# Attention logits of a graph kernel drawn for seven steps at once

## The reference, cut to what matters

```
a = h[src] @ Ws.T + h[dst] @ Wd.T + emb_rel[etype] @ Wr.T
e = leaky_relu((a @ attn_fc2_w.T)[:, 0], 0.01)
m = segment_max(e, dst)
w = exp(e - m[dst])
alpha = w / segment_sum(w, dst)[dst]
agg = segment_sum(alpha[:, None] * h[src], dst)
```

## Time and profile before

| | us |
|---|---|
| median of 3 runs | 11182.82 (11172.02 to 11192.22) |
| the profiled execution | 11168.36 |
| its span, first to last instruction | 11166.6 |
| attention, from its first one-hot to its last addition's start | 7414.1 to 9960.2 |
| attention, steady part | 2527.3 |
| busy in the steady part: TensorE, VectorE, ScalarE, GpSimd | 2308, 2230, 1950, 1547 |

### The profile page before, as it was taken

How to read it: one execution, slowest core, us unless ns; L and a number is a source line. 1 busy time by engine, 2 the same in 40 slices (tenths; PEclk the granted TensorE clock), 3 DMA queues, 4 the chain that set the end, 5 groups by cost and what they waited for, 6 DMA issues and landing times.

```text
span 11166.6 us, 189255 instructions
## 1 busy us (share of the span) xinstructions
PE 8637.6 (77%) x45271; PEld 6646.5 (60%) x45271; DVE 7796.6 (70%) x26977; ACT 6047.5 (54%) x18738; POOL 7800.5 (70%) x7060
## 2 busy tenths in 40 slices
PE   3344555555578899988898999989999999967888
PEld 2233333333346677677777778767777777745665
DVE  5677454455486677755664444778888888889999
ACT  6854555555585666611110000767777777766665
POOL 0088887778718888888865888846666666649995
PEclk6555555555589999999999999975555555557776
DMA  2111111111167888899996777321111111110000
GB/s 47 20 49 41 43 43 44 45 44 43 45 204 196 204 218 218 210 276 246 244 257 223 227 232 223 48 57 46 46 46 46 46 46 46 46 46 6 1 1 24
DMA packets 656014, 1170.95 MB, mean 105 GB/s; under 512 B 140942, under 2 KB 565074, under 8 KB 632158
## 3 DMA queue, kind: packets, MB, share of 16 engines
q0 software_dynamic: 363536, 437.35, 20.4%
q10 hardware_dynamic: 25344, 574.83, 13.4%
q1 hardware_dynamic: 266062, 146.67, 5.2%
HBM read 885.82 MB, written 278.99 MB: 104 GB/s over the span
## 4 chain that ended last, share of the span: by engine, by line
POOL 31%; PE 23%; ACT 15%; issue 14%; DVE 12%; DMA 2%; DVEq 2%; SPq 1%; ACTq 0%; POOLq 0%
POOL step_data L1388 12%; POOL onehot L2075 9%; PE bank L987 8%; PE bank L1349 7%; POOL step_data L1660 6%; ACT onehot L974 5%; POOL gather_ring L1388 4%; ACT onehot L976 3%; DVE step_small L1895 2%; ACT keys L580 2%; PE bank L1935 2%; PE bank L1943 1%; ACT step_small L1972 1%; DVE arena L1883 1%; DVE keys L1908 1%
## 5 line engine op out<-in xcount | busy, mean ns | idle before, releaser
L962 POOL DMA_INDIRECT gather_ring<-mean_rows,step_data x1660 | 2045.0, 1232 | 902.4 <-DVE arena L759 396.9
L987 PE MATMUL bank<-gather_ring,onehot 128*128 128x130 f32 x3320 | 1252.5, 484 | 1244.5 <-ACT onehot L976 490.9
L1349 PE MATMUL bank<-arena 128*128 128x384 bf16 x9506 | 1797.7, 329 | 25.4 <-DMA arena<-split_out 24.2
L987 PEld LDWEIGHTS bank<-gather_ring,onehot 128*128 128x128 f32 x3320 | 833.8, 313 | 1650.5 <-ACT onehot L976 655.5
L1349 PE MATMUL bank<-arena,keys 128*128 128x384 bf16 x9408 | 1791.8, 330 | 9.5 <-DMA arena<-split_im 9.5
L1388 POOL DMA_INDIRECT step_data<-hidden,window_idx x960 | 1553.1, 1618 | 316.6 <-issue 291.5
L1349 PEld LDWEIGHTS bank<-arena 128*128 128x128 bf16 x9506 | 1307.3, 138 | 328.3 <-issue 41.3
L1349 PEld LDWEIGHTS bank<-arena,keys 128*128 128x128 bf16 x9408 | 1294.5, 138 | 318.1 <-issue 34.9
L1660 POOL DMA_INDIRECT step_data<-next_rows,window_idx x672 | 1117.4, 1663 | 344.8 <-issue 313.1
L1020 DVE TENSOR_TENSOR arena<-arena,bank 128x130 f32 x1660 | 480.8, 290 | 1125.8 <-PE bank L987 1027.5
L1866 POOL DMA_INDIRECT gather_ring<-attention_rows,step_data x834 | 786.3, 943 | 605.9 <-DVE step_small L1919 460.7
(11 more groups left out here) (310 smaller groups left out, 20200.2 us busy)
## 6 DMA issues: line engine op xcount, KB each, us to landing
keys<-count_rows ACTq DMA_DIRECT2D x56, 3136.0 KB
arena<-count_rows ACTq DMA_DIRECT2D x56, 3136.0 KB
count_rows<-arena ACTq DMA_DIRECT2D x29, 3136.0 KB
count_rows<-keys ACTq DMA_DIRECT2D x29, 3136.0 KB
gather_ring<-mean_rows,step_data POOLq DMA_INDIRECT x1660, 2.5
step_data<-hidden,window_idx POOLq DMA_INDIRECT x960
gather_ring<-attention_rows,step_data POOLq DMA_INDIRECT x834, 2.5
keys<-attention_rows,step_data POOLq DMA_INDIRECT x826, 2.5
```

The lines of the kernel that those rows point to most:

```text
L962: e.indirect_dma_start(ring_at(rings.slot(name, i), SUM_COLS, SUMS - 1), None, rows, bass.IndirectOffsetOnAxis(src_idx[:, i:i + 1], 0), bo ...
L987: e.matmul(pass_bank[i % N_SUM_BANKS][:, 0:SUMS], onehot[:, i % STEP_SLOTS, :], ring_at(rings.slot(name, i), SUM_COLS, SUMS), start=True, ...
L1349: m = e.matmul(pass_bank[n % 2][:, 0:SPLIT_COLS], counts[t % 2][:, :, h], split[:, h, :], start=(h == 0), stop=(h == NODE_TILES - 1))
```

## The change

Seven steps share one draw of logits. The product of `nodes_hot` (hop 3) has three columns a step, one for each bf16 piece, and goes to the step's own three columns of one PSUM bank that holds the scores of seven steps. After the seventh step's product, `draw_vector` (hop 4, every seventh step) adds the three pieces with one reduction over 128x7x3, adds the relation scores and the source scores of seven steps, and takes the leaky ReLU; the two copies of coefficients stand in it as well. The later stages move back by twelve half-steps (the mask from hop 5 to 17, the addition from 15 to 27), since the first of seven steps now waits for the last. `edges_hot` gets 16 slots. PSUM is divided: the transposes of hop 1 alternate between two banks, the seven steps' scores have one, and the later half of the pipeline (transposes and sums) goes round five; TensorE waits for the copy of two steps back and the addition of five steps back. Gathers signal by groups of seven, and GpSimd waits for the sum of 28 steps back and the coefficients' copies alone. The diff, cut to its core:

```diff
-                             ("attention", GATHER_SLOTS, [1] * STEPS)))
+                             ("attention", ATTENTION_SLOTS // DRAWN,
+                              [min(DRAWN, STEPS - g * DRAWN) for g in range(DRAWS)])))
...
-    HOPS = 16
+    HOPS = 28
+    DRAW_STEPS = 4
+    drawn = small[:, 0:4, 0:DRAWN]
...
+    HALF_BANKS, LATE_BANKS = 2, 5
...
+    def dst_scores(n):
+        return bank_all[HALF_BANKS][:, 0:PIECES * n].rearrange("p (s k) -> p s k", k=PIECES)
...
     def attention_gpsimd(e):
...
-            if j >= GATHER_SLOTS:
-                e.wait_ge(a_logit, 2 * (j - GATHER_SLOTS + 1))
...
+    def draw_vector(e, g):
+        first, end = g * DRAWN, min((g + 1) * DRAWN, STEPS)
+        n, slot, done = end - first, first % ATTENTION_SLOTS, DRAW_STEPS * g
...
+        l = drawn[:, g % 4, 0:n]
+        e.wait_ge(a_score, end)
+        if g >= 4:
+            e.wait_ge(a_masked, (g - 3) * DRAWN)
+        e.tensor_reduce(l, dst_scores(n), AX.X, ALU.add).then_inc(a_logit)
+        e.wait_ge(*rings.landed("attention", g))
+        e.tensor_copy(edge_norm[:, first:end], rows[:, :, D + 3]).then_inc(a_coefs)
+        e.wait_ge(a_logit, done + 1)
+        e.tensor_tensor(l, l, edge_score[:, first:end], ALU.add).then_inc(a_logit)
+        e.wait_ge(a_logit, done + 2)
+        e.tensor_tensor(l, l, rows[:, :, D + 1], ALU.add).then_inc(a_logit)
+        e.tensor_copy(edge_coef[:, first:end], rows[:, :, D + 2]).then_inc(a_coefs)
+        e.wait_ge(a_logit, done + 3)
+        e.scalar_tensor_tensor(l, l, 0.01, l, ALU.mult, ALU.max).then_inc(a_logit)
...
     def attention_vector(e, regs, late_regs):
...
-            if (j := due(now, 4, STEPS, 2)) is not None:
...
-                e.scalar_tensor_tensor(l, dst_score(s), edge_score[:, j:j + 1], row[:, D + 1:D + 2], ALU.add,
-                                       ALU.add).then_inc(a_logit)
-                e.wait_ge(a_logit, 2 * j + 1)
-                e.scalar_tensor_tensor(l, l, 0.01, l, ALU.mult, ALU.max).then_inc(a_logit)
+            if (j := due(now, 4, STEPS, 2)) is not None and (j % DRAWN == DRAWN - 1 or j == STEPS - 1):
+                draw_vector(e, j // DRAWN)
             if (j := due(now, 0, STEPS, 2)) is not None:
                 if j >= STEP_SLOTS:
-                    e.wait_ge(a_added, j - STEP_SLOTS + 1)
+                    e.wait_ge(a_score, j - STEP_SLOTS + 1)
+                if j >= HOT_SLOTS:
+                    e.wait_ge(a_masked, j - HOT_SLOTS + 1)
...
     def attention_tensor(e, regs):
...
-                parts = regs.parts(e, j, *((2 * A_SDST + i, 2 * A_SDST + i + 1) for i in range(PIECES)))
+                parts, = regs.parts(e, j, (2 * A_SDST, 2 * A_SDST + PIECES))
                 e.wait_ge(a_nodes, j + 1)
-                e.matmul(dst_score(s), nodes_hot[:, s, :], parts[0], start=True, stop=False)
-                e.matmul(dst_score(s), nodes_hot[:, s, :], parts[1], start=False, stop=False)
-                e.matmul(dst_score(s), nodes_hot[:, s, :], parts[2], start=False, stop=True).then_inc(a_score)
+                if g and j % DRAWN == 0:
+                    e.wait_ge(a_logit, DRAW_STEPS * (g - 1) + 1)
+                e.matmul(dst_scores(DRAWN)[:, j % DRAWN, :], nodes_hot[:, s, :], parts, start=True,
+                         stop=True).then_inc(a_score)
```

More of the change, by code:

```diff
@@ L84 @@
 DRAWN = 7
+DRAWS = -(-STEPS // DRAWN)
+HOT_SLOTS = 2 * STEP_SLOTS
 class Tally:
@@ L1868, in attention_gpsimd @@
                                  bounds_check=None).then_inc(
-                rings.landed("attention", j)[0], 16)
+                rings.landed("attention", j // DRAWN)[0], 16)
+    def draw_vector(e, g):
+        first, end = g * DRAWN, min((g + 1) * DRAWN, STEPS)
+        n, slot, done = end - first, first % ATTENTION_SLOTS, DRAW_STEPS * g
+        room = gather_ring if slot < GATHER_SLOTS else keys_all[:, STEP_COLS:]
+        rows = room[:, slot % GATHER_SLOTS * ROW_COLS:][:, 0:n * ROW_COLS].rearrange("p (s c) -> p s c", c=ROW_COLS)
+        l = drawn[:, g % 4, 0:n]
[12 more added lines that the diff above has]
+        e.scalar_tensor_tensor(l, l, 0.01, l, ALU.mult, ALU.max).then_inc(a_logit)
     def attention_vector(e, regs, late_regs):
@@ L1875, in attention_vector @@
         for now in steps_due():
-            if (j := due(now, 15, STEPS, 2)) is not None:
+            if (j := due(now, 27, STEPS, 2)) is not None:
                 s = j % STEP_SLOTS
@@ L1882, in attention_vector @@
                     e.wait_ge(a_added, j)
-                e.scalar_tensor_tensor(part, part, step_small[:, s, 3:4], step_sums(s), ALU.mult,
+                e.scalar_tensor_tensor(part, part, step_small[:, s, 3:4], step_sums(j), ALU.mult,
                                        ALU.add).then_inc(a_added)
-            if (j := due(now, 8, STEPS, 2)) is not None:
+            if (j := due(now, 20, STEPS, 2)) is not None:
                 s = j % STEP_SLOTS
@@ L1891, in attention_vector @@
                 e.tensor_tensor(step_small[:, s, 2:3], nmax, step_small[:, s, 1:2], ALU.min).then_inc(a_max)
-            if (j := due(now, 7, STEPS, 2)) is not None:
+            if (j := due(now, 19, STEPS, 2)) is not None:
                 s = j % STEP_SLOTS
                 e.wait_ge(a_logit_turned, j + 1)
[L1895 to L1909, removed]
-            if (j := due(now, 4, STEPS, 2)) is not None:
[L1911 to L1914, removed]
-                e.wait_ge(*rings.landed("attention", j))
-                e.scalar_tensor_tensor(l, dst_score(s), edge_score[:, j:j + 1], row[:, D + 1:D + 2], ALU.add,
-                                       ALU.add).then_inc(a_logit)
-                e.wait_ge(a_logit, 2 * j + 1)
-                e.scalar_tensor_tensor(l, l, 0.01, l, ALU.mult, ALU.max).then_inc(a_logit)
@@ L1930, in attention_tensor @@
         for now in steps_due():
-            if (j := due(now, 14, STEPS, 2)) is not None:
+            if (j := due(now, 26, STEPS, 2)) is not None:
                 s = j % STEP_SLOTS
```

71 lines of the change are left out of this document (40 added, 31 removed).

## The result

| | before | changed |
|---|---|---|
| median, us | 11179.56 (4 runs) | 10995.53 (4 runs, 10992.28 to 10999.00) |
| ratio, 95% interval | | 0.9834 (0.9817 to 0.9851) |
| span of the profiled execution, us | 11166.6 | 10990.5 |
| one-hot to one-hot, mean of 1659 steps, us | 1.530 | 1.416 |

The account below looks back on a forecast made before the run. VectorE was taken to lead the attention's 1.53 us step, with TensorE close behind. Terms -400 + 83 + 52 + 5 sum to -260 us, giving 10,923 us, range 10,770 to 11,110.

Parts of the forecast that it names:

- Steps 1 and 2: VectorE in the attention: removed instructions and moved copies save 548 + 31 us, added draws cost 179; net 400 us saved.
- The rule that the prediction quotes from the Trainium skill: VectorE's next instruction waits until the pipe is empty; by it 464 us saved instead of 400; the prediction did not adopt it.
- Step 4: Attention: VectorE's undisturbed step falls to 1.02 us, but loops at 1.05 and 1.06 hold it at 1.07; 83 us given back.
- The loop through the logits: Attention, from one reduction to the next through mask and TensorE's transpose: 1.05 us, a limit just above VectorE's 1.02.
- Step 5: TensorE's register reloads in the attention lose the slack that hid them: 52 us given back, bounds 0 to 116.
- Step 3: TensorE's three score products become one: at most 0.10 us a step, floor 1.16 to about 1.06, no gain while VectorE leads.
- Step 6: GpSimd's gathers in the attention, 1.25 us each: cost nothing while a step stays over 1.25.
- Step 7: Attention's new bank waits cost nothing; the pipeline, twelve half-steps longer, adds 5 us.
- ScalarE as the bound: Rival: ScalarE's 1.18 us a step binds the attention, 266 us given back, 11,106 us; chance 0.19.
- VectorE alone: Rival: only VectorE decides the attention's step, loops overlap and reloads coincide; 395 us saved, 10,788 us; chance 0.17.
- The clock: Rival: TensorE's granted clock rises from 0.52 in the attention, its loops drop out; 395 us saved, 10,788 us; chance 0.06.

Follow-up runs that it names:

- after_read_early: Changed kernel with VectorE reading the addition's register right behind the mask instead of between one-hot and addition; 10,863.95 us, ratio 0.9770 to the kernel before.
- after_one_wait: Changed kernel with a single wait before the one-hot, on the transposed logits, in place of two; ratio 0.9789 to the kernel before, on a slow chip.
- before_one_product: Kernel before with one product for the score in place of three, two pieces left out; 11,090.60 us, ratio 0.9973.
- after_both: Changed kernel with the addition's register read early and one register table in place of two; ratio 0.9783 to the kernel before, 0.9795 when repeated, on slow chips.

## Why the prediction was right, and where it was wrong

- *Steps 1 and 2, VectorE removed and added: right.* -0.240 us a step from maximum to one-hot, -398 us; -400 was forecast. 0.33 went in the undisturbed step, and a draw costs 0.71 where I took 0.75. The rule that the prediction quotes from the Trainium skill (VectorE: DVE Perf Modes, "The DRAIN you can't avoid") did not decide: L1890 starts 0.09 us behind L1888, which lasts 0.18.
- *Step 4, "VectorE's undisturbed step falls to 1.35 - 0.33 = 1.02 us", failed.* It fell to 1.11. I took each stretch between two starts as a property of that pair and missed that the 0.22 from one-hot to addition held only as long as the sequencer had run ahead. after_read_early and after_one_wait each give back 0.07 of it. The term was +83 for loops through TensorE; the stretch cost +156 (0.085 in each step, 141 us, the rest where a wait for the sum falls on it). These 73 us are as much as the 72 by which 10,923 missed. The mechanism given for the term was wrong too: VectorE's own sequencer keeps the changed kernel's step at 1.11, and no loop through TensorE does. The loop through the logits was put at 1.05, and the step of 1.04 in after_read_early differs from that by no more than the rows are rounded: whether that loop would bind a still shorter step is open.
- *Step 5, TensorE's reloads, +52: right in size, by luck.* Mask to maximum grew by 0.032, +53 us, and only at the reload of the maximum's registers and the step behind. At the reload it is VectorE's own load that starts later: 0.27 us behind the addition (median) and 0.10 before. A second semaphore instruction (L1928) now stands ahead of it; how much TensorE's load at the same place adds is not shown. In the step behind, VectorE waits for ScalarE, which was itself held up by the late maximum:

```profile
8502.06 0.16 DVE L1919 TENSOR_TENSOR step_small<-arena,step_small 128x1 f32<-128x1 f32 x1 [0.32 <-issue]
...
8502.52 0.29 ACT L1991 ACTIVATE step_small<-arena,step_small 128x1 f32 x1 [0.47 <-DVE step_small L1919]
...
8502.85 0.20 ACT L1994 ACTIVATE arena<-step_small 128x1 f32 x1
...
8503.26 0.16 DVE L1919 TENSOR_TENSOR step_small<-arena,step_small 128x1 f32<-128x1 f32 x1
```

  In four of five such steps the maximum starts 0.20 us behind the end of ScalarE's copy (L1994); before, with the longer step, it stood 0.53 behind.
- *Step 3, "Nothing of that lies on the path": nearly, but the saving was mis-sized.* before_one_product puts it at 27 to 33 us, in the step with TensorE's reload, and nothing in the undisturbed ones. TensorE's step fell by 0.06 (1.153 to 1.094) and not by 0.10: its floor is 1.09 and not 1.06, just under VectorE's 1.11.
- *Step 6, gathers: right.* They are released by the sum (570 us of waiting), and the step stayed above 1.25.
- *Step 7, banks and depth:* the drain, from the last one-hot to the last addition, grew by 8 us where 5 was forecast; no wait on a bank appears among the stage's 22 largest waits.
- *Rivals.* ScalarE as the bound at 1.18 a step falls: its L1991 starts come as close as 1.02 us, so its work did pack closer. VectorE alone falls by the +156. The clock did rise a little, from 0.52 to 0.59 in the stage, but gave nothing that shows: steps that lie for the most part at the level of 2.4 GHz average 1.56 us and those at 1.2 GHz 1.39. That alone would not settle it, since the high level falls mostly on the steps around the reloads; but compared position by position among the eight, the steps at 2.4 GHz are no shorter either where they are most frequent (1.40 against 1.40 at one position, 1.32 against 1.20 at the other).

## What to carry to other kernels

When instructions are taken out of a saturated engine's loop, what shrinks is the distance between starts, and part of what was hidden behind the removed ones (semaphore and register operations of the next instruction) appears in the neighbouring distance: add the sequencer's chain of the shortened loop, too. Register loads of 0.6 us on the leading engine are worth removing before arithmetic is: one table in place of two brought 119 us for some twenty lines, on the chip where VectorE leads. Look for the next engine's floor before adding such gains up: here it lies at 1.09, under a step of 1.11, and what VectorE saves beyond comes back in part as waits. Compare such edits on one chip and with the changed kernel beside them; on the slow chips another engine decided, and after_both's edits were worth 6 us. Of the versions tried, one table alone has the lowest ratio (0.9734 against the change's 0.9834, on chips of nearly the same time before, but not the same one); it was not run alone on a slow chip.

## What was unexpected of the hardware

Chips differ by 4.5% on the same program (11,117 and 11,622 us), and the steps show how: VectorE's undisturbed 1.35 us is the same to 0.01, while TensorE stands still between its own instructions.

And the granted clock of a stretch has to be held against the matmuls themselves. For the stretch from 1000 to 3000 us, in the first mean, it is given as 0.50 in the profile before and 1.00 in the profile after, yet the matmuls of that stretch last as long in both:

```profile
L987 PE MATMUL bank<-gather_ring,onehot 128*128 128x130 f32 x2601 | 981.7, 483 | 944.9 <-ACT onehot L976 346.5 <-issue 317.4 <-ACT onehot L974 263.8
...
L990 PE MATMUL bank<-gather_ring,onehot 128*128 128x130 f32 x2588 | 977.8, 483 | 950.8 <-ACT onehot L979 348.0 <-issue 325.9 <-ACT onehot L977 262.8
```

The second half of such a product starts 0.348 us (median) behind the first in both profiles, and in the attention, with nearly the same shape, 0.324 at 0.50 and 0.165 at 1.00. The trace after holds no record of the clock in this stretch. So TensorE ran at 1.2 GHz there both times, and that the stages up to the attention took the same time (7414.1 and 7412.6 us to the first one-hot) says nothing of whether they depend on TensorE's clock.
